# Moving the first half's output transposes behind the second half's first matrix product, in a recurrent layer with a gated feed-forward

## The chip, the cores and the metric

One Trainium2 chip, all 8 cores. Each core runs the same program on its own sequence (one of 8 batch entries), with no traffic between cores. The metric is the device time in microseconds (us) of the slowest core; lower is better.

## What is computed

Per core, for a sequence x of 8192 tokens with 1024 channels each:

```python
xn = layernorm(x)                                   # over channels
Lambda = exp(-exp(nu_log) + 1j * exp(theta_log))
Bu = einsum('ph,blh->blp', (B_re + 1j*B_im) * exp(gamma_log)[:, None], xn)
xs = associative_scan(h_t = Lambda * h_{t-1} + Bu_t)  # along the 8192 tokens
s  = einsum('hp,blp->blh', C_re + 1j*C_im, xs).real + D * xn
g  = silu(relu(xn @ W1 + b1) @ W2 + b2)             # W1 1024x4096, W2 4096x1024
out = x + s * g
```

## The kernel before

The tokens are cut into 16 blocks of 512. The main loop (line 539) runs k from 0 to 16, and is a software pipeline of two stages: iteration k does the recurrence of block k and the feed-forward and output of block k-1. All five engines run their own in-order instruction lists; the order within each is the order in which the Python code emits, and everything between engines goes through counting semaphores. `V(...)` emits on VectorE, `S(...)` on ScalarE, `nc.tensor` on TensorE, `nc.sync` is the queue that issues most DMAs.

One iteration, in the order of the code:

1. Cx (lines 549 to 583): s = C times the scanned states of block k-1, 128 matmuls of 512 columns, which ScalarE copies into `s_b`.
2. Transposes of the normalized tokens of block k into `xnf` (lines 585 to 623).
3. Bu (lines 676 to 707): 128 matmuls of 512 columns. Behind each pair of PSUM banks VectorE runs the recurrence (rotation, `tensor_tensor_scan`, rotation back: lines 715 to 731), a long list of instructions that goes on under the matmuls that follow. `chain_done` (line 742) marks its end. Its temporary `tmp[1]` is the first part of `g_b`.
4. Feed-forward of block k-1 in two halves of 256 tokens, `sub` 0 and 1 (line 765). FFN1 is 4 pieces of `w1` (256 matmuls, lines 770 to 796), evicted with Relu into `h1` by ScalarE; FFN2 is 4 pieces of `w2` (256 matmuls, lines 810 to 839), evicted with Silu into `g_b` (line 834), four outputs from PSUM tensor PA and four from PB. ScalarE waits for `chain_done` before it (line 806), since the scan still uses `g_b`.
5. Gate, lines 846 to 865, on VectorE: four SCALAR_TENSOR_TENSOR and one multiply for each half of the channels, result in `g_b`.
6. Output, lines 867 to 897: for each of four groups TensorE transposes four 128x128 fp32 tiles of `g_b` into one PB bank (line 876), VectorE adds the bank to the input block `xsl` (line 888), and when all four are added ScalarE's queue writes the half block out (line 897).
7. Prefetch and preparation, lines 898 to 907: the sync queue waits for that output DMA, then loads the half of block k+1 into the same buffer (line 901). For `sub` 0 alone VectorE then runs `emit_rot(k+1)` (64 instructions that advance the rotation tables, lines 205 to 212) and `emit_ln_v(k+1, 0)` (layernorm statistics of the newly loaded half block, 7 instructions, lines 222 to 230).

The weights stream from HBM in 2 MB pieces through three slots `wslot`. `pump()` issues the next piece on the sync queue once the piece three before it has been used up. The four PB banks rotate through `pp_acquire` and `pp_release`: a bank is taken again when whoever read it last (ScalarE or VectorE) has finished. FFN2 takes all four at once (line 807).

Of the kernel before, what the change touches and what calls it, by code (L numbers as in the profile page):

```python
# [10 lines left out]
ALU = mybir.AluOpType  # L11

H = 1024
I = 4096
T = 8192
NSUB = 256
NSUP = 512
NSTEP = T // NSUP
# [26 lines left out]
def build_program():  # L45
    nc = bass.Bass("TRN2", target_bir_lowering=False)
# [41 lines left out]
    def psum(name, shape):  # L88
# [10 lines left out]
    g_b = sb("g_b", [128, CH * NSUB], F32)  # L99
    tmp = [tmp0, g_b[:, 0:NSUP]]  # L100
    h1 = sb("h1", [128, CI * NSUB], BF16)
    xsl = [sb(f"xsl{i}", [128, 4 * H], F32) for i in range(2)]
# [10 lines left out]
    ident = sb("ident", [128, 128], F32)  # L113
# [3 lines left out]
    PB = psum("PB", [128, 2048])  # L117
    PP = [PB[:, b * 512:(b + 1) * 512] for b in range(4)]

    TE = Ch(nc, es, "TE")  # L120
    VE = Ch(nc, es, "VE")
# [8 lines left out]
    XS = [[Ch(nc, es, f"XS{i}_{h}", step=16) for h in range(2)]  # L130
          for i in range(2)]
    SYO = [Ch(nc, es, f"SYO{i}", step=16) for i in range(2)]
# [9 lines left out]
    def V(emit):  # L142
        VE.wait(nc.vector)
        return VE.inc(emit())
# [5 lines left out]
    def VX(ch, mark=None):  # L150
        ch.wait(nc.vector, mark)

    def SX(ch, mark=None):
        ch.wait(nc.scalar, mark)

    def TX(ch, mark=None):
        ch.wait(nc.tensor, mark)

    def sbap(t, off, dims):
        return bass.AP(t.tensor if isinstance(t, bass.AP) else t, off, dims)  # L160
# [5 lines left out]
    def x_src_half(k, h):  # L166
        return bass.AP(x_d.ap().tensor, (k * NSUP + h * 256) * H,
                       [[H, 128], [128 * H, 2], [1, H]])

    def out_dst_ap(k, sub):  # L170
        return bass.AP(out_d.ap().tensor, (k * NSUP + sub * NSUB) * H,
                       [[H, 128], [128 * H, 2], [1, H]])

    XEXT = 4 * H
# [4 lines left out]
    def pp_acquire():  # L179
        b = pp_state["i"] % 4  # L180
        kind, mark = pp_state["hist"][b]
        if kind == "SE":
            TX(SE, mark)
        else:
            TX(VE, mark)
        pp_state["i"] += 1
        return b

    def pp_release(b, kind, mark):
        pp_state["hist"][b] = (kind, mark)  # L190
# [91 lines left out]
    out_dma = {}  # L282
# [72 lines left out]
    while L < NSUP:  # L355
        for m in range(CH):
# [6 lines left out]
            sl = tmp0[:, 88 + m:89 + m]  # L363
# [175 lines left out]
    for k in range(NSTEP + 1):  # L539
# [9 lines left out]
        if has_prev:  # L549
# [6 lines left out]
            for m in range(CH):  # L556
                bk = pp_acquire()
                bank = PB[:, bk * 512:bk * 512 + 512]
                first = True
                inst = None  # L560
# [24 lines left out]
        if has_cur:  # L585
# [3 lines left out]
            for sub in range(2):  # L589
                if sub == 1:  # L590
                    TX(SE, m_norm23_of[k])
                for c in range(CH):
                    bk = pp_acquire()
                    inst = None
                    for tbl in range(2):
                        tb = sub * 2 + tbl
# [164 lines left out]
        if has_prev:  # L761
            new_gev = [[0] * 8, [0] * 8]
            resid_done = [0, 0]
            w1p, w2p = cur_w
            for sub in range(2):
                if sub == 0 and st_first_ffn:
                    SX(WST[0])
# [31 lines left out]
                    dump("dbg_h1", h1[:, :], SE, h1_ev_last)  # L799
                if DEBUG and k == 1 and sub == 1:  # L800
                    SX(DBG)

                TX(SE, bu_evac_prev[6])
                TX(SE, bu_evac_prev[7])
# [59 lines left out]
                    tmh[hf] = V(lambda sa=s_ap, ga=g_ap:  # L864
                                nc.vector.tensor_tensor(ga, sa, ga, ALU.mult))  # L865

                rm_last = 0
                for halfc in range(2):
                    for tbl in range(2):
                        tb = sub * 2 + tbl  # L870
                        bk = pp_acquire()
                        TX(VE, tmh[halfc])
                        inst = None
                        for c4 in range(4):
                            c = halfc * 4 + c4
                            inst = nc.tensor.transpose(  # L876
                                PB[:, bk * 512 + c4 * 128:
                                   bk * 512 + c4 * 128 + 128],
                                g_b[:, c * NSUB + tbl * 128:
                                    c * NSUB + tbl * 128 + 128],  # L880
                                ident[:, :])
                        gm = TE.inc(inst)
                        VX(TE, gm)
                        xo = xsl[(k - 1) % 2][:, tb * H + halfc * 512:
                                              tb * H + halfc * 512 + 512]
                        rm = V(lambda a=xo,
                               b2=PB[:, bk * 512:(bk + 1) * 512]:
                               nc.vector.tensor_tensor(a, a, b2, ALU.add))
                        pp_release(bk, "VE", rm)
                        rm_last = rm  # L890

                resid_done[sub] = rm_last
                VE.wait(nc.scalar, rm_last)
                srcx = sbap(xsl[(k - 1) % 2], sub * 2 * H,
                            [[XEXT, 128], [H, 2], [1, H]])
                out_dma[(k - 1, sub)] = SYO[sub].inc(
                    nc.scalar.dma_start(out_dst_ap(k - 1, sub), srcx))
                if k + 1 < NSTEP:
                    sl = (k + 1) % 2
                    SYO[sub].wait(nc.sync)  # L900
                    XS[sl][sub].inc(nc.sync.dma_start(
                        sbap(xsl[sl], sub * 2 * H,
                             [[XEXT, 128], [H, 2], [1, H]]),
                        x_src_half(k + 1, sub)))
                    if sub == 0:
                        emit_rot(k + 1)
                        emit_ln_v(k + 1, 0)
            g_ev = new_gev
            du_last[(k - 1) % 2] = VE.n
            if k + 1 < NSTEP:  # L910
# [55 lines left out]
```

How the kernel before makes its waits and increments, by code:

```python
    def inc(self, inst):  # L34
        inst.then_inc(self.h, self.step)
        self.n += self.step
        return self.n
# [1 line left out]
    def wait(self, eng, mark=None):  # L39
        v = self.n if mark is None else mark
        if v and v > 0:
            eng.wait_ge(self.h, v)
# [464 lines left out]
    def pump():  # L507
        while pend:
            j, kind, q = pend[0]
            if kind in pump_hold:
                return
            if j >= 3:
                um = piece_use_marks[j - 3]
                if um is None:
                    return
                nc.sync.wait_ge(TE.h, um)
            piece_marks[j] = WS[j % 3].inc(
                nc.sync.dma_start(wslot[j % 3][:, :], piece_src(kind, q)))
            pend.pop(0)
```

## Time and profile before

| | |
|---|---|
| median of 2 runs | 3939.38 us (3937.81 to 3940.96) |
| the profiled execution | 3937.43 us, its slowest core's span 3936.4 us |
| spans of the 8 cores | 3916.0 to 3936.4 us |
| busy share of the span | TensorE 77%, VectorE 56%, ScalarE 28% |
| mean granted TensorE clock, cores 0 to 7 | 0.89 to 0.895 of full speed |
| DMA moved, slowest core | 801 MB, 203 GB/s on average |

The profile page lists busy times, groups of instructions by line, and the chain of work that ended last, followed back from the last instruction. The trace behind it can be asked for the instructions of a stretch in order of time, with the idle time before each group and what ended it. All rows below are of core 0, the slowest.

### The profile page before, as it was taken

Reading aid. Unit: us, or ns where it says so; the run is one execution under the profiler, and the core shown is the slowest. Engines: PE = TensorE matmul, PEld = TensorE weight load, DVE = VectorE, ACT = ScalarE, POOL = GpSimd, SP = SyncE. Lnnn points to the kernel's source line nnn. Section 1 sums busy time; section 2 is a strip of 40 time slices with the busy share of each in tenths; the row PEclk is TensorE's granted clock in tenths of the full one; section 3 lists DMA queues with packets and bytes.
Section 4 is the critical chain, followed back from the end, with each engine's and each line's share of the span. In section 5 each row is a group of like instructions: output and inputs, shape, how many; then the busy total and the mean of one; then the engine's idle time right before and its main releaser. Section 6 shows DMA issues by size and latency. Waiting matters only on the chain.

```text
span 3936.4 us, 62467 instructions; the slowest of 8 cores (3916.0 to 3936.4 us)
## 1 busy us (share of the span) xinstructions
PE 3012.0 (77%) x21664; PEld 2218.6 (56%) x21760; DVE 2196.1 (56%) x4122; ACT 1114.6 (28%) x2022; POOL 22.0 (1%) x46
## 2 busy tenths in 40 slices
PE   2401497888887897878787888878787888878798
PEld 1201266574756666564756666574756666565667
DVE  5680075564838475564838375564838385665401
ACT  3201232323322323323322323323222323323222
POOL 0010000000000000000000000000000000000000
PEclk9855698989898998988898998988898998989899
DMA  5776477574756767574757777574757766574776
GB/s 143 188 155 143 121 224 236 162 240 159 249 185 221 224 212 243 171 239 152 247 176 229 222 223 226 172 237 159 246 171 236 231 215 217 179 251 161 233 226 214
DMA packets 409237, 800.99 MB, mean 203 GB/s; under 512 B 50528, under 2 KB 50528, under 8 KB 406880
## 3 DMA queue, kind: packets, MB, share of 16 engines
q1 hardware_dynamic: 361184, 738.26, 59.2%
q10 hardware_dynamic: 41984, 41.95, 3.1%
q0 software_dynamic: 5760, 16.78, 2.9%
q8 instruction: 180, 2.95, 0.3%
q14 instruction: 129, 1.06, 0.1%
HBM read 755.01 MB, written 58.72 MB: 207 GB/s over the span
## 4 chain that ended last, share of the span: by engine, by line
PE 44%; DVE 34%; DMA 8%; issue 7%; ACT 6%; DVEq 1%; ACTq 1%; SPq 0%; POOLq 0%; POOL 0%
PE PB L780 13%; PE PB L563 12%; PE PA L820 6%; PE PB L820 5%; DVE g_b L654 4%; DVE tmp L649 4%; DVE s_b L851 3%; DMA h<-W 3%; PE PB L694 3%; DMA sc_w<-h 2%; DVE xsre L664 2%; DVE vv L670 2%; DVE vv L666 2%; DVE vv L672 2%; DVE g_b L865 2%
## 5 line engine op out<-in xcount | busy, mean ns | idle before, releaser
L780 PE MATMUL PB<-xnf,wslot 128*128 128x256 bf16 x8192 | 948.5, 280 | 64.9 <-DMA wslot<-sc_w 64.9
L780 PEld LDWEIGHTS PB<-xnf,wslot 128*128 128x128 bf16 x8192 | 824.5, 101 | 188.6 <-issue 69.5
L790 ACT ACTIVATE h<-PB,b_tab 128x256 bf16<-128x256 f32 x1024 | 485.7, 474 | 637.6 <-PE PB L780 614.4
L820 PE MATMUL PA<-h,wslot 128*128 128x256 bf16 x4096 | 467.9, 272 | 44.4 <-ACT h L790 44.1
L820 PE MATMUL PB<-h,wslot 128*128 128x256 bf16 x4096 | 468.1, 273 | 0.0
L820 PEld LDWEIGHTS PA<-h,wslot 128*128 128x128 bf16 x4096 | 398.4, 98 | 98.4 <-issue 52.7
L820 PEld LDWEIGHTS PB<-h,wslot 128*128 128x128 bf16 x4096 | 400.7, 98 | 46.4
L851 DVE SCALAR_TENSOR_TENSOR s_b<-xnf,d_tab,s_b 128x256 f32<-128x256 bf16 x256 | 124.0, 484 | 519.8 <-ACT g_b L834 495.7
L876 PE MATMUL PB<-ident,g_b 128*128 128x128 f32 x512 | 104.6, 372 | 328.8 <-DVE g_b L865 328.8
L425 PE MATMUL PB<-ident,s_b 128*128 128x128 f32 x256 | 62.1, 424 | 309.3 <-ACT s_b L417 218.3
L876 PEld LDWEIGHTS PB<-ident,g_b 128*128 128x128 f32 x512 | 83.9, 193 | 345.9 <-issue 345.9
L694 PE MATMUL PB<-xnf,wslot 128*128 128x512 bf16 x1008 | 235.2, 394 | 56.5 <-ACT xnf L617 30.6
L563 PE MATMUL PB<-xsre,wslot 128*128 128x512 bf16 x976 | 251.9, 397 | 33.2 <-DMA wslot<-sc_c 25.1
L563 PE MATMUL PB<-xsim,wslot 128*128 128x512 bf16 x1024 | 242.3, 379 | 0.0
L717 DVE TENSOR_TENSOR xsre<-vv,cS 128x512 bf16<-128x512 bf16 x128 | 88.6, 692 | 273.5 <-ACT vv L705 261.5
L425 PEld LDWEIGHTS PB<-ident,s_b 128*128 128x128 f32 x256 | 50.2, 223 | 320.9 <-issue 320.9
L245 DVE RECIPROCAL carry<-carry 128x2 f32<-128x2 f32 x32 | 5.3, 166 | 402.9 <-ACT carry L243 402.8
L694 PE MATMUL PA<-xnf,wslot 128*128 128x512 bf16 x992 | 224.6, 379 | 1.7
L694 PEld LDWEIGHTS PB<-xnf,wslot 128*128 128x128 bf16 x1024 | 102.2, 101 | 184.1 <-issue 74.2
L563 PEld LDWEIGHTS PB<-xsre,wslot 128*128 128x128 bf16 x1024 | 104.1, 102 | 159.3 <-issue 51.0
L834 ACT ACTIVATE g_b<-PA,b_tab 128x256 f32<-128x256 f32 x128 | 60.7, 474 | 415.1 <-PE PA L820 410.4
L834 ACT ACT_TABLE_LOAD x15 | 19.2, 1283 | 561.1 <-DVE xsim L674 561.1
(86 smaller groups left out, 2903.3 us busy)
## 6 DMA issues: line engine op xcount, KB each, us to landing
wslot<-sc_w SPq DMA_DIRECT2D x256, 2048.0 KB, 11.4
wslot<-sc_b SPq DMA_DIRECT2D x32, 2048.0 KB, 11.8
wslot<-sc_c SPq DMA_DIRECT2D x32, 2048.0 KB, 12.1
xsl<-x SPq DMA_DIRECT2D x32, 1024.0 KB, 5.6
out<-xsl ACTq DMA_DIRECT2D x32, 1024.0 KB, 5.1
h<-W POOLq DMA_DIRECT2D x8, 1024.0 KB, 14.7
sc_w<-h SPq DMA_DIRECT2D x8, 1024.0 KB, 8.4
h<-W POOLq DMA_DIRECT2D x32, 256.0 KB, 4.6
```

Source lines behind the costliest of these rows:

```text
L425: inst = nc.tensor.transpose(PB[:, bb * 512 + (j % 4) * 128: bb * 512 + (j % 4) * 128 + 128], bt_s[pp][:, j * 128:j * 128 + 128], ident[:, :])
L563: inst = nc.tensor.matmul(bank, pslot(cpiece)[:, kk * 1024 + m * 128: kk * 1024 + (m + 1) * 128], xsbuf[:, kk * NSUP:(kk + 1) * NSUP], sta ...
L649: nc.vector.tensor_tensor_scan(a, d0, d1, carry[:, 2 * mm:2 * mm + 1], ALU.mult, ALU.add))
L654: nc.vector.tensor_tensor_scan(a, d0, d1, carry[:, 2 * mm + 1:2 * mm + 2], ALU.mult, ALU.add))
L694: inst = nc.tensor.matmul(reg, pslot(bj)[:, kk * 1024 + m * 128: kk * 1024 + (m + 1) * 128], xnf_k[:, kk * NSUP:(kk + 1) * NSUP], start=(k ...
L717: nc.vector.tensor_tensor(a, b, c2, ALU.mult))
L780: inst = nc.tensor.matmul(bank[:, 0:256], pslot(jw)[:, kk * 1024 + ml * 128: kk * 1024 + (ml + 1) * 128], xnf_p[:, kk * NSUP + sub * NSUB: ...
L790: ev = S(lambda m2=mi, b=bank: nc.scalar.activation(h1[:, m2 * NSUB:(m2 + 1) * NSUB], b[:, 0:256], AF.Relu, bias=b1_tab[:, m2:m2 + 1]))
L820: inst = nc.tensor.matmul(w2bank[m], pslot(jw)[:, kl * 1024 + m * 128: kl * 1024 + (m + 1) * 128], h1[:, (q * 8 + kl) * NSUB: (q * 8 + kl ...
L834: nc.scalar.activation(g_b[:, mm * NSUB:(mm + 1) * NSUB], bnk, AF.Silu, bias=b2_tab[:, mm:mm + 1]))
L851: nc.vector.scalar_tensor_tensor(s_b[:, m2 * NSUP + sub * NSUB: m2 * NSUP + sub * NSUB + NSUB], xnf_p[:, m2 * NSUP + sub * NSUB: m2 * NSUP ...
L876: inst = nc.tensor.transpose(PB[:, bk * 512 + c4 * 128: bk * 512 + c4 * 128 + 128], g_b[:, c * NSUB + tbl * 128: c * NSUB + tbl * 128 + 12 ...
```

## The change

The body of item 6 and 7 above becomes a function `emit_outT(sub2, tmh2)`, unchanged in itself. For `sub` 1 it is called where it stood. For `sub` 0 it is no longer called after the gate; the marks of the gate are kept in `tmh_a`, and the call is made in the next pass of the `sub` loop, between FFN1 and FFN2 of `sub` 1. With it go the transposes and adds of `sub` 0, its output DMA, the load of the first half of block k+1, `emit_rot(k+1)` and `emit_ln_v(k+1, 0)`. Where the diff is cut inside the function, the transposes, the add and the two source patterns read as in lines 876 to 895 and 902 to 904.

```diff
+            tmh_a = [0, 0]
+
+            def emit_outT(sub2, tmh2):
+                rm_last = 0
+                for halfc in range(2):
+                    for tbl in range(2):
+                        tb = sub2 * 2 + tbl
+                        bk = pp_acquire()
+                        TX(VE, tmh2[halfc])
...
+                        gm = TE.inc(inst)
+                        VX(TE, gm)
...
+                        pp_release(bk, "VE", rm)
+                        rm_last = rm
+                resid_done[sub2] = rm_last
+                VE.wait(nc.scalar, rm_last)
...
+                out_dma[(k - 1, sub2)] = SYO[sub2].inc(
+                    nc.scalar.dma_start(out_dst_ap(k - 1, sub2), srcx))
+                if k + 1 < NSTEP:
+                    sl = (k + 1) % 2
+                    SYO[sub2].wait(nc.sync)
...
+                    if sub2 == 0:
+                        emit_rot(k + 1)
+                        emit_ln_v(k + 1, 0)
+
             for sub in range(2):
...
+                if sub == 1:
+                    emit_outT(0, tmh_a)
 
                 TX(SE, bu_evac_prev[6])
                 TX(SE, bu_evac_prev[7])
...
-                rm_last = 0
-                for halfc in range(2):
-                    for tbl in range(2):
...
-                        emit_rot(k + 1)
-                        emit_ln_v(k + 1, 0)
+                if sub == 0:
+                    tmh_a = tmh
+                else:
+                    emit_outT(1, tmh)
```

## Rows read from the trace of the kernel before

**Rows 1.** The page: span, and the chain that ended last by engine.

```profile
span 3936.4 us, 62467 instructions; the slowest of 8 cores (3916.0 to 3936.4 us)
PE 44%; DVE 34%; DMA 8%; issue 7%; ACT 6%; DVEq 1%; ACTq 1%; SPq 0%; POOLq 0%; POOL 0%
```

**Rows 2.** The page, groups of instructions: busy, mean ns | idle before, releaser.

```profile
L876 PE MATMUL PB<-ident,g_b 128*128 128x128 f32 x512 | 104.6, 372 | 328.8 <-DVE g_b L865 328.8
L834 ACT ACT_TABLE_LOAD x15 | 19.2, 1283 | 561.1 <-DVE xsim L674 561.1
```

**Rows 3.** Timeline of TensorE, k = 8: start, duration, work [idle before it].

```profile
2131.26 3.66 PE L820 MATMUL PB<-h,wslot 128*128 128x256 bf16 x32
2150.81 1.94 PE L876 MATMUL PB<-ident,g_b 128*128 128x128 f32 x8 [15.89 <-DVE g_b L865]
2154.49 1.94 PE L876 MATMUL PB<-ident,g_b 128*128 128x128 f32 x8 [1.74 <-DVE g_b L865]
2156.23 29.01 PE L780 MATMUL PB<-xnf,wslot 128*128 128x256 bf16 x256
2186.64 3.65 PE L820 MATMUL PA<-h,wslot 128*128 128x256 bf16 x32 [1.41 <-ACT h L790]
...
2215.78 1.07 PE L876 MATMUL PB<-ident,g_b 128*128 128x128 f32 x8 [1.03 <-DVE g_b L865]
...
2223.31 3.17 PE L563 MATMUL PB<-xsre,wslot 128*128 128x512 bf16 x7 [1.92 <-DMA wslot<-sc_c]
```

**Rows 4.** Timeline of ScalarE, same iteration.

```profile
2143.44 1.28 ACT L834 ACT_TABLE_LOAD   x1 [37.39 <-DVE xsim L674]
...
2147.01 2.17 ACT L834 ACTIVATE g_b<-PB,b_tab 128x256 f32<-128x256 f32 x4
...
2211.41 0.47 ACT L834 ACTIVATE g_b<-PA,b_tab 128x256 f32<-128x256 f32 x1 [0.40 <-PE PA L820]
```

**Rows 5.** Timeline of VectorE, same iteration.

```profile
2154.45 3.06 DVE L888 TENSOR_TENSOR xsl<-xsl,PB 128x512 f32<-128x512 f32 x4
2157.62 0.35 DVE L205 TENSOR_SCALAR tmp<-sS,sD 128x256 f32<-128x256 f32 x1
...
2195.03 0.17 DVE L230 TENSOR_SCALAR carry<-tmp 128x2 f32<-128x2 f32 x1
2212.06 2.25 DVE L851 SCALAR_TENSOR_TENSOR s_b<-xnf,d_tab,s_b 128x256 f32<-128x256 bf16 x4 [16.86 <-ACT g_b L834]
```

**Rows 6.** Stretches: length, busy of PE, PEld, DVE, ACT, POOL, granted clock, DMA share, GB/s.

```profile
2143.00:2147.00 4.00, 0.00 (x0) 0.00 (x0) 0.26 (x1) 3.18 (x5) 0.00 (x0) 0.50 0.00 0
2158.00:2159.00 1.00, 1.00 (x11) 0.89 (x10) 0.81 (x2) 0.47 (x1) 0.00 (x0) 0.97 0.53 217
2226.00:2228.00 2.00, 2.00 (x10) 0.83 (x9) 0.00 (x0) 1.91 (x2) 0.00 (x0) 0.92 0.93 377
2178.00:2208.00 30.00, 28.59 (x263) 25.40 (x261) 13.91 (x32) 4.28 (x10) 0.00 (x0) 1.00 0.97 289
```

**Rows 7.** The page, DMA issues: count, KB each, median us to landing.

```profile
xsl<-x SPq DMA_DIRECT2D x32, 1024.0 KB, 5.6
out<-xsl ACTq DMA_DIRECT2D x32, 1024.0 KB, 5.1
```

**Rows 8.** Timeline of TensorE: transposes of k = 1, then k = 14.

```profile
607.83 1.94 PE L876 MATMUL PB<-ident,g_b 128*128 128x128 f32 x8 [15.74 <-DVE g_b L865]
...
672.88 1.06 PE L876 MATMUL PB<-ident,g_b 128*128 128x128 f32 x8 [1.03 <-DVE g_b L865]
...
3475.08 1.94 PE L876 MATMUL PB<-ident,g_b 128*128 128x128 f32 x8 [15.95 <-DVE g_b L865]
...
3540.10 1.07 PE L876 MATMUL PB<-ident,g_b 128*128 128x128 f32 x8 [1.03 <-DVE g_b L865]
```

**Rows 9.** Timeline of TensorE, the last iteration, k = 16.

```profile
3858.82 1.06 PE L876 MATMUL PB<-ident,g_b 128*128 128x128 f32 x8 [1.04 <-DVE g_b L865]
...
3864.24 30.02 PE L780 MATMUL PB<-xnf,wslot 128*128 128x256 bf16 x256
```

More of the change, by code:

```diff
@@ L764, in build_program @@
             w1p, w2p = cur_w
+            tmh_a = [0, 0]
[6 more added lines that the diff above has]
+                        TX(VE, tmh2[halfc])
+                        inst = None
+                        for c4 in range(4):
+                            c = halfc * 4 + c4
+                            inst = nc.tensor.transpose(
+                                PB[:, bk * 512 + c4 * 128:
+                                   bk * 512 + c4 * 128 + 128],
+                                g_b[:, c * NSUB + tbl * 128:
+                                    c * NSUB + tbl * 128 + 128],
+                                ident[:, :])
+                        gm = TE.inc(inst)
+                        VX(TE, gm)
+                        xo = xsl[(k - 1) % 2][:, tb * H + halfc * 512:
+                                              tb * H + halfc * 512 + 512]
+                        rm = V(lambda a=xo,
+                               b2=PB[:, bk * 512:(bk + 1) * 512]:
+                               nc.vector.tensor_tensor(a, a, b2, ALU.add))
+                        pp_release(bk, "VE", rm)
+                        rm_last = rm
+                resid_done[sub2] = rm_last
+                VE.wait(nc.scalar, rm_last)
+                srcx = sbap(xsl[(k - 1) % 2], sub2 * 2 * H,
+                            [[XEXT, 128], [H, 2], [1, H]])
+                out_dma[(k - 1, sub2)] = SYO[sub2].inc(
[3 more added lines that the diff above has]
+                    SYO[sub2].wait(nc.sync)
+                    XS[sl][sub2].inc(nc.sync.dma_start(
+                        sbap(xsl[sl], sub2 * 2 * H,
+                             [[XEXT, 128], [H, 2], [1, H]]),
+                        x_src_half(k + 1, sub2)))
+                    if sub2 == 0:
+                        emit_rot(k + 1)
+                        emit_ln_v(k + 1, 0)
             for sub in range(2):
@@ L865, in build_program @@
                                 nc.vector.tensor_tensor(ga, sa, ga, ALU.mult))
-                rm_last = 0
-                for halfc in range(2):
-                    for tbl in range(2):
[L870 to L905, printed above, removed]
-                        emit_rot(k + 1)
-                        emit_ln_v(k + 1, 0)
+                if sub == 0:
+                    tmh_a = tmh
+                else:
+                    emit_outT(1, tmh)
             g_ev = new_gev
```

## The prediction, made before the changed kernel was run

> **What bounds the kernel now.** I read the page first, then the timelines of TensorE, ScalarE and VectorE over one iteration, then the granted clock and the DMA share of short stretches. The page's chain goes through TensorE and VectorE in turn [rows 1]: neither is the bound by itself, so the question in each stage is who is waited for. The largest idle time of TensorE stands ahead of the output transposes, 328.8 us over 64 waits, and in 15 iterations what ScalarE waited for before the Silu of the first half was the last instruction of VectorE's scan chain [rows 2].
>
> One iteration shows it. FFN2 of sub 0 ends on TensorE at 2131.26 + 3.66 = 2134.9. VectorE's scan ends at 2143.4 and only then ScalarE loads its table and runs the eight Silus, the four PA banks first, then the PB banks from 2147.01 [rows 4]. The gate ends at 2154.3, the transposes run at 2150.81 and 2154.49, and FFN1 of sub 1 begins at 2156.23 [rows 3, 5]. VectorE then does four adds (to 2157.5), `emit_rot` and `emit_ln_v` (2157.62 to 2195.03 + 0.17 = 2195.2, thus 37.6 us) and is idle for 16.86 us until the fourth Silu of sub 1 lets the second gate begin at 2212.06 [rows 5]. Ahead of the tail TensorE waits 1.03 us [rows 3]. Here the two engines are near balance: the tail is set by TensorE, with 16.9 us in hand on VectorE.
>
> **The change, part by part.**
>
> *The start of FFN1 of sub 1.* It needs weights and a free PB bank. All issued weights have landed, since the DMA share is 0.00 at 2143 to 2147 [rows 6]. The first bank is free when the first PB Silu ends, 2147.01 + 0.47 = 2147.5 (2.17 us are four Silus with their gaps) [rows 4]; with 0.15 for the hand-over, FFN1 starts at 2147.65 and not at 2156.23, 8.6 us earlier. The rest of the 15.9 us wait, 12.7 us, stays: it belongs to the scan chain and the Silus, which the change does not touch. The later banks come free every 0.57 us, faster than one group of 8 matmuls uses them (29.01 / 32 = 0.91).
>
> *Its length.* Before, 29.01 us, with the clock at its lower level (1.2 GHz) until about 2158.0, 1.8 us after the first matmul [rows 3, 6]; that cost 0.9, so at 2.4 GHz it is 28.1. Now the matmuls follow directly on the idle time. In the rows the clock rose 3.0 us after Cx began (2223.31; 0.92 over 2226 to 2228 means about 2226.3), and 7.2 us after the first transposes of sub 0, 3.5 us after the second ones, which ran on into matmuls [rows 3, 6]. I take 4.0 us at half rate, between 3.0 and 7.2, since the start here is dense: it costs 2.0 (1.5 to 3.6). FFN1 lasts 30.1 and ends at 2177.75, 7.5 us earlier than 2185.24.
>
> *The transposes between FFN1 and FFN2.* Eight transposes took 1.07 us at full clock [rows 3], four about 0.53. With 0.2 for the hand-over VectorE's first add starts 0.75 us after FFN1, and four adds take 3.06 [rows 5]: they end at 2181.55. FFN2 takes all four PB banks at once, so it waits for the last add and starts at about 2181.8. Before it came 1.4 us behind FFN1, now 4.05: 2.65 us of a new wait. FFN2 is 4.8 us earlier than 2186.64.
>
> *What goes with them.* `emit_rot` and `emit_ln_v`, 37.6 us, now start behind the adds at 2181.65 instead of 2157.62: 24.0 us later. This is the part that decides. They stand in VectorE's list ahead of the gate of sub 1. They end at 2219.25, and the gate, ready at 2207.2 on TensorE's side (the fourth Silu ended 25.2 us after FFN2 began: 2211.88 less 2186.64 [rows 3, 4]), starts at 2219.3. Cross-check: 24.0 later less the 16.86 that VectorE was idle gives 7.2. So the tail comes **7.2 us later** per iteration, though FFN2 ended 4.8 us earlier, at 2209.9. TensorE then idles about 13 us ahead of the last transposes.
>
> *The rest of the tail.* Gate, transposes, adds, and Cx of the next iteration follow as before, only relative to the gate. TensorE is now at half clock there, so the last transposes take the 1.94 of [rows 3] at 2150.81 rather than 1.07; only the second batch is on the path, and it was mostly at half clock already. The wait of 1.92 us for a piece of C ahead of Cx [rows 3] disappears where it occurred. I set the two against each other: 0, between -1.9 and +0.5.
>
> *DMA and queues.* The output DMA of sub 0 is issued at 2181.6 and takes 5.1, the load of x after it 5.6 [rows 7]; x is there at about 2193, and is needed by `emit_ln_v` at 2215. The sync queue now waits for that output behind the issue of the third w2 piece of sub 1, and holds back the fourth until about 2187; its slot is free only when the first w2 piece is used up, 2181.8 + 7.0 = 2188.8, so nothing is held. The 2 MB of output and input now fall in a stretch whose DMA share was already 0.97 at 289 GB/s [rows 6]: 2.1 MB at that rate is 7.3 us of delay for the weights. It is covered: FFN2 may run 12 us late before the gate notices (2219.3 less 2207.2). If the cover were gone, the 7.3 would be on the path. ScalarE waits for the last add before it issues the output DMA, with only FFN2's Silus behind it, 22 us away.
>
> *Iterations.* The transposes of k = 1 to 14 show one pattern: from the first of sub 0 to the first of sub 1 65.05 us in k = 1, 64.97 here, 65.02 in k = 14 [rows 3, 8]. They are 14, and only in them do `emit_rot` and `emit_ln_v` run. Against this iteration the others are 0.1 nearer to my end, so 7.1 each: 14 x 7.1 = 99.
>
> In k = 15 the two are absent, so the gate follows FFN2: -8.6 + 1.1 + 2.65 = -4.9. In k = 16 there is no scan, and the Silus are done as FFN2 ends: FFN1 of sub 1 starts at 3858.82 - 1.04 = 3857.8 instead of 3864.24 (-6.4), lasts 28.1 instead of 30.02 because TensorE doesn't stop (-1.9), and pays the 2.65: -5.7 [rows 9]. Together -10.6.
>
> *Sum.* 3937.4 (the profiled execution's own time, 2 us under the median) + 99 - 10.6 = 4025.8, **4026 us**, 2.2% over the median of 3939.4.
>
> **The rivals.**
>
> *A, the forecast: VectorE's list delays the tail.* By the uncertain terms (length of the half-clock stretch, hand-overs, the wait for C), 5.6 to 8.8 us per iteration: 3926.8 + 78 to 3926.8 + 123, 4005 to 4050. For it: 37.6 us of work in 25.4 us of cover. Chance 0.80. Measurements of this kernel tell about 2% from no change, that is 4018; 0.24 of the 0.80 lies below it.
>
> *B, faster: the 37.6 us stay hidden.* Then the time follows TensorE: -4.8 in 14 iterations and -10.6, 3860 us. The condition is at the gate of sub 1: VectorE must be free by 2207.2, thus `emit_rot` and `emit_ln_v` must take under 25.5 us. The rows give 37.6, without idle time among them [rows 5], so chance 0.04. The Trainium skill, "Perfetto Trace Analysis", Identifying Performance Opportunities, tells one to improve the most-contended engine, the one of highest occupancy; by that, feeding TensorE (77% busy against VectorE's 56%) sooner would give this rival's result, and the rows of this stretch speak against it.
>
> *C, slower still by the clock.* With TensorE idle for 13 us ahead of the tail, Cx runs longer at 1.2 GHz. It was low for 3.0 us of Cx here; another 3 us would cost 1.5 per iteration: 4026 + 21 = 4047. For it: the longer idle time. Against: after 15.9 us idle FFN1 of sub 1 was low for only 1.8 us behind its transposes [rows 3, 6]. Chance 0.08. The Trainium skill, "TensorE: Matmul & The Clock Gate", Part 4: PE-mode transpose, says that transposes don't count as busy for the clock as matmuls do; that would make C the result. The 1.8 us against the 3.0 of Cx suggest that here they help.
>
> *D, slower still by DMA.* The output, the input and the weights crowd each other in FFN2 of sub 1 beyond the 12 us of cover, or x lands after 2215. Half of the 7.3 us beyond it would be 14 x 3.7 = 51: 4077. Against: 22 us in hand for x. Chance 0.06.
>
> *E, about no change:* FFN1 gains nothing and the tail loses nothing, because some wait pairs them in another way; nothing in the rows shows such a wait. 3939, chance 0.02.
>
> **How the numbers follow.** The predicted time is A's, 4026. A's bounds give 4005 to 4050; outside lie B, D, E and about 0.06 of A and C, under 0.2 in all. Slower by over 2%: 0.56 of A, C and D, 0.70. Within 2%: 0.24 of A and E, 0.26. Faster: B, 0.04.
>
> **What would show it.** In a middle iteration: TensorE's idle time ahead of FFN1 of sub 1 is about 12.7 us and released by a Silu; FFN1 ends 7.5 us earlier relative to the end of the scan; four adds stand between FFN1 and FFN2, with 4 us between the two; VectorE runs without idle time from these adds to the gate of sub 1, whose 16.86 us of idle time is gone; TensorE idles about 13 us ahead of the last transposes, released by VectorE. Iterations k = 1 to 14 are each about 7 us longer. The forecast is wrong if VectorE still waits ahead of the second gate, if `emit_ln_v` waits for x, or if FFN2 of sub 1 waits for weights for more than 12 us.

## The result: 2.3% slower, and where the time went

The changed kernel takes 4026.1 us (median of 11 runs), the kernel before 3938.1 us (median of 10 beside it); the ratio is 1.0227 with a 95% interval of 1.0195 to 1.0259: slower, and by about 2%, the lower end lying just under it. Some executions of every kernel here ran several per cent longer, with the cores of one die at a lower granted clock; all ratios leave them out, and "no interval" below means that too few of the others were left. The predicted time was 4026 us. That it agrees to the microsecond is luck, as the terms below show; the mechanism is the predicted one.

The page of the changed kernel, of its slowest core (core 3): span, busy time of TensorE and VectorE, the chain that ended last by engine, and three groups of instructions with their idle time and releaser.

```profile
span 4022.3 us, 62563 instructions; the slowest of 8 cores (4005.9 to 4022.3 us)
PE 3044.5 (76%) x21760; PEld 2226.9 (55%) x21760; DVE 2195.8 (55%) x4122; ACT 1114.6 (28%) x2022; POOL 22.0 (1%) x46
DVE 40%; PE 36%; issue 8%; DMA 7%; ACT 6%; DVEq 2%; ACTq 1%; SPq 0%; POOL 0%; POOLq 0%
...
L824 PE MATMUL PB<-xnf,wslot 128*128 128x256 bf16 x8192 | 956.5, 282 | 254.1 <-ACT g_b L880 206.5
L866 PE MATMUL PA<-h,wslot 128*128 128x256 bf16 x4096 | 494.4, 282 | 59.5 <-DVE xsl L789 34.5
L777 PE MATMUL PB<-ident,g_b 128*128 128x128 f32 x512 | 89.5, 340 | 191.4 <-DVE g_b L911 191.4
```

VectorE's busy time is what it was, but its share of the chain rose from 34% to 40% and TensorE's fell from 44% to 36% [rows 1]. In place of the 328.8 us that TensorE waited ahead of its output transposes [rows 2] stand three waits that add up to 432: 206.5 us ahead of FFN1 of sub 1, released by a Silu, 191.4 us ahead of the transposes, nearly all of it in the tail (the stretch from the Silus of sub 1 to the next Cx), and 34.5 us ahead of FFN2, released by the moved adds.

One iteration (k = 8, on core 3, the scan ending at 2195.0 and ScalarE's table load following at 2195.24). Timeline of TensorE: start, duration, work [idle before it].

```profile
2182.08 3.66 PE L866 MATMUL PB<-h,wslot 128*128 128x256 bf16 x32
2199.41 29.82 PE L824 MATMUL PB<-xnf,wslot 128*128 128x256 bf16 x256 [13.68 <-ACT g_b L880]
2229.07 1.95 PE L777 MATMUL PB<-ident,g_b 128*128 128x128 f32 x16
2233.27 5.32 PE L866 MATMUL PA<-h,wslot 128*128 128x256 bf16 x32 [2.25 <-DVE xsl L789]
2238.43 3.66 PE L866 MATMUL PB<-h,wslot 128*128 128x256 bf16 x32
...
2256.94 3.65 PE L866 MATMUL PA<-h,wslot 128*128 128x256 bf16 x32 [0.88 <-DMA wslot<-sc_w]
2260.43 3.66 PE L866 MATMUL PB<-h,wslot 128*128 128x256 bf16 x32
2274.42 1.94 PE L777 MATMUL PB<-ident,g_b 128*128 128x128 f32 x8 [10.34 <-DVE g_b L911]
2278.11 1.94 PE L777 MATMUL PB<-ident,g_b 128*128 128x128 f32 x8 [1.75 <-DVE g_b L911]
2279.84 2.70 PE L563 MATMUL PB<-xsre,wslot 128*128 128x512 bf16 x8
```

And the timeline of VectorE in the same iteration:

```profile
2198.88 2.25 DVE L897 SCALAR_TENSOR_TENSOR s_b<-xnf,d_tab,s_b 128x256 f32<-128x256 bf16 x4 [3.83 <-ACT g_b L880]
...
2229.85 3.06 DVE L789 TENSOR_TENSOR xsl<-xsl,PB 128x512 f32<-128x512 f32 x4 [23.71 <-PE PB L777]
2233.02 0.35 DVE L205 TENSOR_SCALAR tmp<-sS,sD 128x256 f32<-128x256 f32 x1
...
2266.61 0.69 DVE L222 BATCH_NORM_STATS2 tmp<-xsl 128x6 f32<-128x512 f32 x1
...
2270.43 0.17 DVE L230 TENSOR_SCALAR carry<-tmp 128x2 f32<-128x2 f32 x1
2270.70 2.25 DVE L897 SCALAR_TENSOR_TENSOR s_b<-xnf,d_tab,s_b 128x256 f32<-128x256 bf16 x4
```

Two lines tell the story. VectorE's last one has no idle time in brackets: the gate of sub 1 starts when the statistics end, where it had waited 16.86 us for a Silu [rows 5]. In its place VectorE now idles 23.71 us under FFN1, ahead of the adds, where it used to rotate tables. From gate to gate it takes 2270.70 - 2198.88 = 71.82 us now; before, it took 2212.06 - 2147.08 = 64.98. The first of these gates in the kernel before (timeline of VectorE, core 0):

```profile
2147.08 2.25 DVE L851 SCALAR_TENSOR_TENSOR s_b<-xnf,d_tab,s_b 128x256 f32<-128x256 bf16 x4 [3.83 <-ACT g_b L834]
```

For all kernels below I read the same four marks in twelve middle iterations of one core, given in brackets. It is the slowest of the profiled execution or within 0.3 us of it, but for "before (3)", "before, rotation late" and "own temporary"; in the last two it is one of the cores that ended earlier. The marks are the first Cx matmul, the first Bu matmul, and the first Silu of each half. The means, in us:

| kernel (core) | Cx to Bu | Bu to first Silu, sub 0 | first Silu, sub 0 to sub 1 | first Silu, sub 1 to next Cx | iteration |
|---|---|---|---|---|---|
| before (3) | 41.7 | 101.6 | 64.3 | 12.3 | 219.9 |
| before (0) | 41.7 | 101.4 | 64.4 | 13.1 | 220.5 |
| changed (3) | 41.8 | 101.7 | 60.9 | 22.8 | 227.2 |
| rotation split (6) | 42.0 | 101.9 | 62.3 | 12.9 | 219.0 |
| changed, no rotation (7) | 42.1 | 101.9 | 61.7 | 12.9 | 218.5 |
| whole rotation back (7) | 41.8 | 101.6 | 71.1 | 12.6 | 227.1 |
| before, rotation late (7) | 41.6 | 102.9 | 64.6 | 23.7 | 232.7 |
| before, no rotation (1) | 41.8 | 101.9 | 64.3 | 12.5 | 220.5 |
| early transposes (3) | 42.1 | 101.9 | 62.9 | 12.6 | 219.5 |
| late load of x (4) | 42.4 | 101.8 | 58.7 | 15.9 | 218.7 |
| late statistics (3) | 42.6 | 101.4 | 59.4 | 15.6 | 219.1 |
| own temporary (3) | 42.2 | 83.7 | 64.0 | 12.2 | 202.0 |
| own temporary, early transposes (2) | 42.2 | 86.0 | 62.1 | 12.6 | 202.9 |
| the same, late load of x (5) | 42.5 | 86.3 | 58.3 | 14.6 | 201.8 |
| the same, late statistics (5) | 42.7 | 86.7 | 58.8 | 14.0 | 202.1 |

The change gains 3.4 us where it was aimed (64.3 to 60.9) and loses 10.5 us in the tail (12.3 to 22.8).

### The profile page after: what moved, and what is told of

Same layout as the page of the kernel before. It is cut to its first block, busy times and chain, and to the rows that moved or that the text cites. A ratio compares the mean times of both kernels' runs of the same rounds, so it can differ in the third digit from the quotient of the medians.

```text
span 4022.3 us, 62563 instructions; the slowest of 8 cores (4005.9 to 4022.3 us)
## 1 busy us (share of the span) xinstructions
PE 3044.5 (76%) x21760; PEld 2226.9 (55%) x21760; DVE 2195.8 (55%) x4122; ACT 1114.6 (28%) x2022; POOL 22.0 (1%) x46
## 4 chain that ended last, share of the span: by engine, by line
DVE 40%; PE 36%; issue 8%; DMA 7%; ACT 6%; DVEq 2%; ACTq 1%; SPq 0%; POOL 0%; POOLq 0%
PE PB L824 14%; PE PB L563 11%; DVE tmp L649 3%; DVE g_b L654 3%; PE PB L694 3%; DMA h<-W 3%; DVE cS L209 3%; DVE sS L212 3%; DMA sc_w<-h 2%; DVE tmp L205 2%; DVE tmp L207 2%; PE PA L694 2%; DVE vv L666 2%; DVE vv L672 2%; DVE xsre L664 2%
## 5 line engine op out<-in xcount | busy, mean ns | idle before, releaser
L824 PE MATMUL PB<-xnf,wslot 128*128 128x256 bf16 x8192 | 956.5, 282 | 254.1 <-ACT g_b L880 206.5
L866 PE MATMUL PA<-h,wslot 128*128 128x256 bf16 x4096 | 494.4, 282 | 59.5 <-DVE xsl L789 34.5
L866 PEld LDWEIGHTS PA<-h,wslot 128*128 128x128 bf16 x4096 | 411.6, 101 | 126.0 <-issue 67.1
L789 DVE TENSOR_TENSOR xsl<-xsl,PB 128x512 f32<-128x512 f32 x128 | 87.9, 687 | 394.2 <-PE PB L777 382.1
L425 PE MATMUL PB<-ident,s_b 128*128 128x128 f32 x256 | 62.1, 424 | 308.7 <-ACT s_b L417 216.1
L777 PE MATMUL PB<-ident,g_b 128*128 128x128 f32 x512 | 89.5, 340 | 191.4 <-DVE g_b L911 191.4
L563 PEld LDWEIGHTS PB<-xsre,wslot 128*128 128x128 bf16 x1024 | 105.3, 103 | 151.8 <-issue 42.6
## 6 DMA issues: line engine op xcount, KB each, us to landing
wslot<-sc_w SPq DMA_DIRECT2D x256, 2048.0 KB, 10.6
wslot<-sc_b SPq DMA_DIRECT2D x32, 2048.0 KB, 10.6
h<-W POOLq DMA_DIRECT2D x8, 1024.0 KB, 14.6
```

Source lines behind the costliest of these rows:

```text
L425: inst = nc.tensor.transpose(PB[:, bb * 512 + (j % 4) * 128: bb * 512 + (j % 4) * 128 + 128], bt_s[pp][:, j * 128:j * 128 + 128], ident[:, :])
L563: inst = nc.tensor.matmul(bank, pslot(cpiece)[:, kk * 1024 + m * 128: kk * 1024 + (m + 1) * 128], xsbuf[:, kk * NSUP:(kk + 1) * NSUP], sta ...
L777: inst = nc.tensor.transpose(PB[:, bk * 512 + c4 * 128: bk * 512 + c4 * 128 + 128], g_b[:, c * NSUB + tbl * 128: c * NSUB + tbl * 128 + 12 ...
L824: inst = nc.tensor.matmul(bank[:, 0:256], pslot(jw)[:, kk * 1024 + ml * 128: kk * 1024 + (ml + 1) * 128], xnf_p[:, kk * NSUP + sub * NSUB: ...
L866: inst = nc.tensor.matmul(w2bank[m], pslot(jw)[:, kl * 1024 + m * 128: kl * 1024 + (m + 1) * 128], h1[:, (q * 8 + kl) * NSUB: (q * 8 + kl ...
```

## Experiments

In the diffs `emit_rot(kk, m0, m1)` does the table chunks m0 to m1 - 1 of 8. Two theories stood against each other. A: VectorE's in-order list (37.6 us of rotation and statistics ahead of the gate of sub 1) sets the tail. D: the moved transposes, their new wait, and the output and input DMAs crowding the weights do.

### Half of the rotation back

The changed kernel, with the rotation split around the adds:

```diff
                     if sub2 == 0:
-                        emit_rot(k + 1)
+                        emit_rot(k + 1, 4, CH)
                         emit_ln_v(k + 1, 0)
...
                 if sub == 0:
                     tmh_a = tmh
+                    if k + 1 < NSTEP:
+                        emit_rot(k + 1, 0, 4)
```

> The changed kernel, with one difference: the first half of the 64 rotation instructions runs on VectorE right after the gate of sub 0 (where VectorE idles for 23.7 us), the second half stays behind the moved adds. Theory A (VectorE's list of 37.6 us ahead of the second gate delays the tail): 16.8 + 4.0 us now stand ahead of that gate, under the 25 us that FFN2 gives, so the tail follows TensorE again, about 3 to 5 us per iteration earlier than in the kernel before: 3860 to 3895 us. VectorE idles again ahead of the second gate, TensorE waits about 1 us ahead of the last transposes. Rival D (the moved transposes, the new wait ahead of FFN2 and the output and input DMAs crowding the weights cost the time): these all stay as in the changed kernel, so the time stays near 4026.

Measured: ratio to the kernel before 0.9943 (0.9922 to 0.9965), 3912.8 us in the profiled execution. Everything of D is still there, and the time is 0.6% under that of the kernel before: A holds, D falls as the cause of the loss. The tail is back at 12.9 us. VectorE waits again ahead of the second gate (timeline of VectorE, split kernel):

```profile
2200.18 0.17 DVE L230 TENSOR_SCALAR carry<-tmp 128x2 f32<-128x2 f32 x1
2207.22 2.25 DVE L897 SCALAR_TENSOR_TENSOR s_b<-xnf,d_tab,s_b 128x256 f32<-128x256 bf16 x4 [6.87 <-ACT g_b L880]
```

But the gain was expected to be 3 to 5 us per iteration, and is 2 between the Silus: 3860 to 3895 was a miss. The next lines are from TensorE's timeline of the same kernel.

```profile
2145.14 30.64 PE L824 MATMUL PB<-xnf,wslot 128*128 128x256 bf16 x256 [16.10 <-ACT g_b L880]
2175.62 2.01 PE L777 MATMUL PB<-ident,g_b 128*128 128x128 f32 x16
2179.82 5.32 PE L866 MATMUL PA<-h,wslot 128*128 128x256 bf16 x32 [2.19 <-DVE xsl L789]
2184.97 3.66 PE L866 MATMUL PB<-h,wslot 128*128 128x256 bf16 x32
```

FFN2's first 32 matmuls take 5.32 us where such a group takes 3.65: they begin at the lower clock. That is 1.7 us per iteration which the sum did not have. FFN1 took 30.6 us in this iteration, but 30.2 in the mean of 15, as in the sum (30.1).

### No rotation at all

> The changed kernel without the rotation of the tables in the main loop (emit_rot is left out there, so the outputs from the third block on are not the reference's); everything else, the moved transposes and DMAs included, stays. Theory A: only 4 us of VectorE work are left ahead of the second gate, and the tail follows TensorE: the same as the split, 3860 to 3895 us. Rival D: near 4026, since VectorE's rotation would not be what is waited for.

Measured: ratio 0.9928 (0.9911 to 0.9946), 3908.0 us in the profiled execution. This kernel leaves the rotation of the tables out, so it only prices it. Taking all 33.5 us away brings hardly more than moving half of them. So the split already hides them (the two intervals overlap), and 0.7% is all that the changed order of TensorE is worth as it stands. The estimate was as high as for the split, for the same reason.

The same instructions taken out of the kernel before:

> The kernel before without the rotation of the tables in the main loop (emit_rot is left out there, so the outputs from the third block on are not the reference's). It prices the 33.5 us of rotation where they stood. Theory A: they were fully hidden there, behind FFN1 and FFN2 of sub 1 with 16.9 us in hand, so taking them away changes nothing: 3935 to 3942 us. If VectorE's total work counted wherever it stands, 14 times some part of 33.5 us would be gained.

Measured: ratio 0.9991 (0.9966 to 1.0017), 3938.4 us in the profiled execution, as expected. The rotation costs nothing measurable in the kernel before and about 115 us in the changed one (4023.4 against 3908.0 in the profiled executions). It is the same work; only its place in VectorE's list differs.

### The rotation late, and nothing else

The kernel before, with `emit_rot` and `emit_ln_v(k+1, 0)` taken out of the tail of sub 0 and put behind FFN1 of sub 1:

```diff
+                if sub == 1 and k + 1 < NSTEP:
+                    VX(TE, TE.n)
+                    emit_rot(k + 1)
+                    emit_ln_v(k + 1, 0)
```

> The kernel before, with transposes, adds and DMAs of sub 0 where they were; only emit_rot and emit_ln_v(k+1, 0) of VectorE wait until FFN1 of sub 1 has ended. Theory A: 37.6 us start at 2185.3 instead of 2157.6 of the iteration read, less the 16.9 us that VectorE idled, so the tail comes 10.9 us later in 14 iterations: 3938 + 153 = about 4090 us. Rival D (moving the transposes and DMAs is what costs): no change, 3938.

Measured: ratio 1.0474 (1.0408 to 1.0541), the lowest run 4111.0 us against the 4090 expected. The order alone, with no transposes moved, costs more than the whole change. The profiled execution took 4163.7 us, with the clock of all cores lower than elsewhere (0.848 to 0.877). The tail, 23.7 us, is close to the expected 12.5 + 10.9; what the row has beyond that is mostly 1.3 us more in Bu to the Silus (102.9), for which no cause is shown.

### The whole rotation back

```diff
                     if sub2 == 0:
-                        emit_rot(k + 1)
                         emit_ln_v(k + 1, 0)
...
                 if sub == 0:
                     tmh_a = tmh
+                    if k + 1 < NSTEP:
+                        emit_rot(k + 1)
```

> The changed kernel, with the whole rotation back right after the gate of sub 0, ahead of the moved adds; transposes, adds, output, load of x and emit_ln_v stay moved. Theory A, VectorE's order decides: the rotation now ends about 41 us after the gate began, some 10 us after the transposes are done, so the adds come late and FFN2 of sub 1 waits for them, about 13 us of idle time of TensorE between FFN1 and FFN2. FFN2 then starts about 4.7 us later than in the kernel before, plus up to 2 us for the clock: 3990 to 4025 us. Rival B (it would have been enough to leave the rotation where it was): 3860 to 3895. Rival D: near 4026 or above.

Measured: ratio 1.025 (1.0172 to 1.0329), 4020.6 us in the fastest run, which lies in A's range, 4027.3 in the profiled one, which lies 2 us above it. Leaving the rotation at about its old time would have been no better than moving it. TensorE's timeline shows the same list delaying another stage:

```profile
2193.82 30.52 PE L823 MATMUL PB<-xnf,wslot 128*128 128x256 bf16 x256 [12.10 <-ACT g_b L879]
2224.18 1.96 PE L777 MATMUL PB<-ident,g_b 128*128 128x128 f32 x16
2237.66 6.32 PE L865 MATMUL PA<-h,wslot 128*128 128x256 bf16 x32 [11.52 <-DVE xsl L789]
```

The adds stand behind 33.5 us of rotation, so FFN2 waits 11.5 us for them. The tail is short again (12.6), and 64.3 has become 71.1. Part of the excess is again the clock: the first group of FFN2 takes 6.32 us, 2.7 more than at full clock.

### Transposes ahead of the last quarter of FFN1

If the 2.2 us of waiting and the half clock ahead of FFN2 are what the split kernel lacks, the transposes should stand where matmuls follow them. Split 3 to 5, and:

```diff
                 for q in range(4):
+                    if sub == 1 and q == 3:
+                        emit_outT(0, tmh_a)
                     jw = w1p[sub][q]
...
-                if sub == 1:
-                    emit_outT(0, tmh_a)
```

> The split kernel (part of the rotation after the gate of sub 0, here the first 3 of 8 table chunks), with the moved transposes one piece earlier: ahead of the last quarter of FFN1 of sub 1 and not behind it. The four adds then run under matmuls, and FFN2 has only the Relu of FFN1 to wait for. Theory: in the split kernel each iteration loses about 4.3 us between FFN1 and FFN2 (2.65 us more of waiting, and 1.7 us because the first matmuls of FFN2 then run at half clock); both go: 14 x 4.3 = 60 and 2 more iterations without rotation, against the 3912 of the fastest split run: about 3850 us. Rival: the half clock at the start of FFN2 and the delay come from the transposes or the DMA traffic themselves and only move along: 3900 to 3915.

Measured: ratio 0.9927 (0.9906 to 0.9948), lowest run 3907.2 us. The expected 3850 was missed, and the time is in the rival's range, though by another wait than the rival named. TensorE's timeline:

```profile
2167.62 1.91 PE L777 MATMUL PB<-ident,g_b 128*128 128x128 f32 x16
2169.37 7.33 PE L826 MATMUL PB<-xnf,wslot 128*128 128x256 bf16 x64
2178.10 3.65 PE L866 MATMUL PA<-h,wslot 128*128 128x256 bf16 x32 [1.41 <-ACT h L836]
...
2195.42 5.32 PE L866 MATMUL PA<-h,wslot 128*128 128x256 bf16 x32 [3.19 <-DMA wslot<-sc_w]
```

The step itself did what it should in this iteration: no wait behind the transposes, FFN2 1.4 us after FFN1 and at full clock. But TensorE then waits 3.19 us for the third piece of w2, and loses 1.7 us to the clock there. In total it waits 48.3 us for weights in FFN2, against 14.9 in the split kernel. The sync queue says why:

```profile
2124.89 43.33 SPq L518 DMA_DIRECT2D wslot<-sc_w  x5
2181.19 0.37 SPq L801 DMA_DIRECT2D xsl<-x  x1
2181.65 4.04 SPq L518 DMA_DIRECT2D wslot<-sc_w  x2
```

A slot was free when FFN1 ended at 2176.7, but the queue stood at its wait for the output DMA until 2181.2 and issued the weights only behind the load of x, 5 us late.

### The load of x later

So the wait and the load go behind the first quarter of FFN2, with `emit_ln_v` behind them:

```diff
                     piece_done(jw, gm)
+                    if sub == 1 and q == 0:
+                        emit_xload(0)
```

> The kernel with the split rotation and the transposes ahead of the last quarter of FFN1, and one difference: the sync queue's wait for the output DMA of sub 0 and the load of x (with emit_ln_v behind it) are issued after the first quarter of FFN2, when that output has long landed. Theory (the sync queue's wait for the output held back the next w2 pieces, and TensorE waited 3.2 us for the third of them, then ran 1.7 us longer at half clock): the 48 us of waits for weights in FFN2 and their half clock go, 3912 - 48 - 20 = about 3845 us. Rival (the DMA engines themselves are full, since output and input crowd the weights wherever they are issued): 3900 to 3915, with the same waits for wslot in FFN2.

Measured: 3901.7 us in the lowest and profiled run (beside a kernel before whose lowest was 3939.9; no interval). The waits for weights in FFN2 fell from 48.3 to 4.0 us, and first Silu to first Silu is 58.7, 5.6 us less than in the kernel before. The expected 3845 was missed again: what was won between the Silus (62.9 to 58.7) went for the most part into the tail, which grew from 12.6 to 15.9. VectorE's timeline:

```profile
2186.91 0.69 DVE L222 BATCH_NORM_STATS2 tmp<-xsl 128x6 f32<-128x512 f32 x1 [7.86 <-DMA xsl<-x]
...
2191.00 2.25 DVE L904 SCALAR_TENSOR_TENSOR s_b<-xnf,d_tab,s_b 128x256 f32<-128x256 bf16 x4
```

Now x arrives late, and the statistics that wait for it stand ahead of the gate. The last step takes them out of the way, behind the adds of sub 1:

```diff
-                    if sub2 == 0:
-                        emit_ln_v(k + 1, 0)
...
                 else:
                     emit_outT(1, tmh)
+                    if k + 1 < NSTEP:
+                        emit_ln_v(k + 1, 0)
```

> The kernel with the late load of x (split rotation, transposes ahead of the last quarter of FFN1), and one difference: the layernorm statistics of the newly loaded half, emit_ln_v(k+1, 0), come behind the gate and the output adds of sub 1 in VectorE's list. In its predecessor VectorE waited for x 7.9 us and the 4 us of statistics then pushed the second gate: from the first Silu of sub 1 to the next Cx took 15.5 us on average where the kernel before took 12.7. Theory: that stretch is back at 12.7, 14 x 2.8 = 39 us less than the 3902 to 3910 of the predecessor: about 3865 us. Rival (pieces of C come late too, DMA is full there): 3885 to 3905, with waits for sc_c ahead of Cx.

Measured: 3909.0 us in the lowest and profiled run, against 3939.7 of the kernel before (no interval). The theory that x was the wait falls. The rival named the right wait, though 3909 lies 4 us above its range: with VectorE out of the way the tail is still 15.6 us. TensorE's timeline shows what is waited for:

```profile
2192.73 1.07 PE L777 MATMUL PB<-ident,g_b 128*128 128x128 f32 x8 [1.04 <-DVE g_b L916]
2196.42 1.06 PE L777 MATMUL PB<-ident,g_b 128*128 128x128 f32 x8 [2.62 <-DVE g_b L916]
2202.69 3.57 PE L563 MATMUL PB<-xsre,wslot 128*128 128x512 bf16 x8 [5.21 <-DMA wslot<-sc_c]
```

Cx waits 5.2 us for its weights. The DMA issues of this kernel: count, KB each, median us to landing.

```profile
wslot<-sc_w SPq DMA_DIRECT2D x256, 2048.0 KB, 11.3
wslot<-sc_b SPq DMA_DIRECT2D x32, 2048.0 KB, 13.9
wslot<-sc_c SPq DMA_DIRECT2D x32, 2048.0 KB, 16.8
xsl<-x SPq DMA_DIRECT2D x32, 1024.0 KB, 13.4
```

The median of 13.4 us for x, where it was 5.6 [rows 7], mixes two halves. Taken apart in the trace, the late load of the first half takes 16.7 us in the median (5.9 in the changed kernel), that of the second half, which was not moved, 4.8 in both. When the late one is issued, two weight pieces (4.2 MB) issued before it are still under way in the median. The pieces of C take 16.8 us (12.1 in the kernel before).

Each time a wait was removed, the next DMA came late: weights, then x, then C. Delivery is what TensorE waits for next in the stretch from FFN1 of sub 1 to Cx, where the DMA share is 0.82 to 0.99 (2140 to 2200 in this kernel). It is no bound on the iteration as a whole: from 2120 to 2140, around the end of the scan, the share is 0.19, and the kernels of the next section move the same 801 MB in 3650 us. Whether a late piece is slow because the DMA engines can give no more, or because it stands behind two others in one queue, was not separated.

### The scan's temporary out of the Silus' way

The 12 us that TensorE still idles ahead of FFN1 of sub 1 belong to `chain_done`: `tmp[1]` lies in `g_b`, which the Silus overwrite. `xn_tok` is not in use during the scan and can hold it. With that, ScalarE's wait is without a cause and goes. The split is 3 to 5, the transposes stand as in the changed kernel.

```diff
-    tmp = [tmp0, g_b[:, 0:NSUP]]
+    tmp = [tmp0, xn_tok[:, 0:2 * NSUP].bitcast(F32)]
...
-                SX(VE, chain_done)
```

> The split kernel (3 of 8 chunks of the rotation first), and the scan's second temporary lies in xn_tok instead of g_b, so that ScalarE's Silu of sub 0 need not wait for the end of the scan (that wait is dropped, its cause being gone). Theory: the 12.7 us which TensorE still idles ahead of FFN1 of sub 1, plus the time up to the first Silus, vanish; the tail comes 15 to 18 us per iteration earlier than in the kernel before, in 15 iterations: 3938 - 15 x 17 = about 3680 us. If the DMA engines, whose share is 0.97 in these stages, can't deliver the weights without the pause: TensorE waits for wslot instead and the time is 3720 to 3800.

Measured: ratio 0.9339 (0.9267 to 0.941), lowest run 3665.6 us. The time from Bu to the first Silu fell from 101.9 us in the split kernel to 83.7, and an iteration takes 17.9 us less than in the kernel before on the same core, where 15 to 18 were expected. With the transposes ahead of the last quarter of FFN1 as well:

> Both together: temporary in xn_tok, transposes ahead of the last quarter of FFN1, the first chunk of the rotation after the gate and seven behind the adds. Theory: about 3 us per iteration less than the kernel with the temporary alone where TensorE is the bound, about 3650 us; the same time as that kernel where DMA or VectorE (41 us of work between the end of the scan and the second gate, against 41.7 us of cover) is the bound.

Measured: ratio 0.9292 (0.9272 to 0.9312), 3656.9 us in the lowest run: 7.1% faster than the kernel before. Against the kernel with the temporary alone the gain is not clear of noise. The temporary was not tried on the kernel before by itself; against the split kernel it takes off 6% (0.9339 against 0.9943). TensorE's timeline of this kernel has no idle time between FFN2 of sub 0 and FFN1 of sub 1:

```profile
2210.19 3.66 PE L865 MATMUL PB<-h,wslot 128*128 128x256 bf16 x32
2213.69 21.12 PE L826 MATMUL PB<-xnf,wslot 128*128 128x256 bf16 x192
2234.65 1.91 PE L777 MATMUL PB<-ident,g_b 128*128 128x128 f32 x16
2236.39 7.15 PE L826 MATMUL PB<-xnf,wslot 128*128 128x256 bf16 x64
```

The late load of x and the late statistics were tried on it too:

> The same difference on the kernel with the scan's temporary in xn_tok and one chunk of the rotation first. Theory: its 34 us of waits for weights in FFN2, with their half clock, go: 3658 - 34 - 14 = about 3610 us. Rival (DMA engines full; without the pause of 12.7 us there is less slack than in the other kernel): 3640 to 3660.

> The same difference on the kernel with the scan's temporary in xn_tok: from the first Silu of sub 1 to the next Cx took 14.6 us there against 12.7. Theory: 14 x 1.9 = 27 us less than 3649: about 3622 us. Rival (DMA full): 3640 to 3650.

Measured: 3649.2 us in the lowest run for the first (kernel before 3939.9 in its lowest run; no interval), 3657.4 in the lowest run for the second with a ratio of 0.9273 (0.9244 to 0.9302). Neither is measurably better than the kernel without them: what they win between the Silus (62.1 to 58.3) comes back in the tail (12.6 to 14.6) and in the remainder. Both theories expected more. The first time is in the rival's range (3640 to 3660), the second 7 us above its range (3640 to 3650); that DMA delivery holds them is in keeping with this, and not shown further.

## Why the prediction was right, point by point

*Start of FFN1.* Predicted 0.15 us after the first PB Silu, with 12.7 us of idle time left. In the iteration shown FFN1 starts 4.17 us after ScalarE's table load does (2199.41 less 2195.24), as forecast (2147.65 less 2143.44 is 4.21); the idle time varies with the end of FFN2 (13.68 here, 206.5 us over 15 iterations, 13.8 on average).

*Its length.* 30.1 predicted, 29.82 measured here, 29.45 to 30.53 over the 15 iterations of this core, 30.0 on average.

*Transposes, adds, FFN2.* FFN2 was to start 4.05 us behind FFN1: 2233.27 less 2229.23 is 4.04. What the sum did not have is that FFN2 then starts at half clock: 5.32 us for its first group instead of 3.65. So TensorE idles 10.3 us ahead of the last transposes here and mostly 11.4, where about 13 were forecast. Under VectorE's list this costs nothing.

*The step that decides.* 37.6 us of VectorE work behind the adds: 2233.02 to 2270.60 is 37.6, with no idle time. The gate comes 71.82 us after the gate of sub 0; the forecast was 64.98 + 7.2 = 72.2. The experiments bear it out from both sides: half of the list moved back removes the loss, all of it moved alone causes it, and where nothing waits behind it, it costs nothing.

*The length of an iteration.* Predicted 7.1 us longer. On core 3 the first transposes of sub 1 are at 683.77 and, thirteen iterations later, at 3636.36, thus 227.1 us each; before, on the same core, at 667.50 and 3524.91, 219.8 us each. That is 7.3; over the eight cores it is 6.8 to 7.6, 7.2 in the mean.

*The last iterations, -10.6.* On core 3 from those transposes of k = 14 to the last ones of all takes 378.1 us (before 384.8): -6.7. Here the start of FFN2 counts: at full clock in the sum, at half clock in the trace, 1.7 us in each of the two iterations, 3.4 together. But on five of the eight cores FFN2 of k = 16 started at full clock (3.65 us), and over all eight the same difference is -6.4 to -15.4, -10.9 in the mean.

*DMA.* Output and input were to crowd the weights by up to 7.3 us under 12 us of cover. TensorE waited 0.88 us for weights in FFN2 here, and 0.9 in the whole run. The prediction had the fourth piece of w2 not held back at all; its slot was free at 2242.1, and the queue, behind its wait for the output DMA, issued the load of x at 2242.86 and the piece at 2243.33. The output DMA took 7.2 us in the median instead of 5.1 [rows 7]; the load of x was in time, since the first BATCH_NORM_STATS2 has no idle time.

*The start, and the sum.* On core 3 the first tail came 16.3 us later than before (683.77 less 667.50), of which 7.2 are the change; on core 0 the same difference is 0.3 (673.15 less 672.88). Over the eight cores it is -4.6 to 16.3, 5.4 in the mean. What is more or less than 7.2 arose ahead of the main loop's steady part; nothing here explains it. Added up in the mean of the eight cores: 5.4 for the first tail, 93.7 for the next thirteen iterations, -10.9 for the rest, to the end of the program, 88.2 us in all (mean span 3925.7 before, 4013.8 changed), where the forecast had 99 - 10.6 = 88.4. A single core is off by much more (73.4 on core 0, 104.7 on core 3), and the slowest core, which the time goes by, was core 0 before and core 3 after: 4022.3 less 3936.4 is 85.9. So the forecast of the mean is borne out term by term, and its agreement with the slowest core to a microsecond is luck.

*The rivals.* B (faster, because feeding the busier engine sooner pays) had its condition named in VectorE's list, and the split kernel meets that condition: it is then faster, though by 0.6% and not by 2%. Nor is TensorE plainly the busier engine: 77% are its matmuls, while its weight loads are busy for 2218.6 us, 56%, as VectorE is (2196.1 us). C, a longer half clock in Cx, did not come: the first eight Cx matmuls take 2.70 us here and 3.17 for seven in [rows 3]. D, crowding by DMA, would have cost 3.7 us an iteration, and TensorE's waits for weights in FFN2 came to 0.9 us in the whole run; the split kernel keeps D's traffic and has no loss. E is excluded by the measured ratio.

## What to carry to other kernels

When an instruction group is moved later on one engine, list what moves with it on the others, and find the next instruction in each of those lists that somebody waits for. Here 5 us on TensorE (FFN2 34.4 us after the first gate instead of 39.6) were bought with the 23.6 us by which VectorE's list slid (34.1 us after the first gate instead of 10.5), past 16.9 us of idle time. Filler work that is free in one idle window should be cut to the size of the windows; half before and half after cost nothing, the whole in either place cost 2.3 to 2.5%. And the larger prize stood next to it: a wait that exists only because two stages share a buffer (6% of the split kernel's time).

## What the runs showed that was not expected

**The clock falls in a short gap behind transposes.** TensorE's granted clock in the changed kernel (stretch: length, busy of PE, PEld, DVE, ACT, POOL, granted clock, DMA share, GB/s):

```profile
2203.00:2204.00 1.00, 1.00 (x11) 0.90 (x10) 0.79 (x3) 0.47 (x1) 0.00 (x0) 1.00 0.00 0
2230.00:2233.00 3.00, 1.02 (x10) 0.73 (x7) 2.60 (x4) 0.14 (x1) 0.00 (x0) 1.00 0.97 298
2233.00:2236.00 3.00, 2.73 (x15) 2.09 (x16) 2.38 (x6) 0.00 (x0) 0.00 (x0) 0.61 1.04 345
2236.00:2237.00 1.00, 1.00 (x7) 0.69 (x6) 0.86 (x2) 0.00 (x0) 0.00 (x0) 0.50 0.84 268
2237.00:2240.00 3.00, 3.00 (x29) 2.65 (x28) 2.36 (x7) 0.00 (x0) 0.00 (x0) 0.98 1.04 418
```

After 30 us of matmuls, 1.95 us of transposes and 2.25 us of idle time TensorE fell from 2.4 to 1.2 GHz, some 0.4 us into FFN2, and stayed there for about 3.4 us (the 0.61, 0.50 and 0.98 above). Between FFN1 and FFN2 of the kernel before, 1.41 us of idle time without transposes had no such effect [rows 3]; nor had 1.91 us of transposes with matmuls right behind them in the kernel with early transposes. The Trainium skill, "TensorE: Matmul & The Clock Gate", Part 4: PE-mode transpose, says that transposes don't count as busy as matmuls do. The fall agrees with it; the rise does not clearly: FFN1 directly behind idle time had the full clock after 3.4 us (2 x the 1.72 by which its 29.82 exceeds 28.1), and FFN1 behind transposes rose 3.5 us after the second batch of them began [rows 3, 6]. The other traces separate transposes from idle time. Over all cores of all kernels of this document, FFN2 (or a later piece of it) began 382 times behind 2.1 to 2.4 us of idle time with transposes ahead of that, and its first group ran partly at the lower clock in 350 of them; with matmuls ahead of the same idle time it did so in 5 of 28. Idle time alone does it too when it is longer: behind 3.19 us of waiting for weights the group took 5.32 us in the kernel with early transposes.

**The same 1 MB load takes 6 or 17 us** depending on what is under way when it is issued. The load of the first half of x lands after 5.9 us in the median in the changed kernel, with one weight piece under way, and after 16.7 in the kernel with late statistics, with two; the load of the second half, issued as before, takes 4.8 in both.
